# Forming du*B of five scan units on GpSimd instead of TensorE, with their decays in PSUM

## What is computed

```python
x = einsum('bld,ed->bel', ctx, in_proj_w)             # 256 channels
u = silu(conv4(x) + conv_b)                           # causal, 4 taps, by channel
dt_low, B, C = split(einsum('bdl,ed->bel', u, x_proj_w), [8, 24])   # 8 + 16 + 16 rows
dt = softplus(dt_low @ dt_proj_w + dt_proj_b);  A = -exp(A_log)
state = state * exp(dt * A) + (dt * u) * B            # 16 states a channel, 256 steps
y = sum_n(state * C) + D * u;  y = y * silu(layernorm(x))
x = x + tanh(g0) * y.T
xq = quant(layernorm(x));  x1, x3 = split(xq @ w13.T)     # 2 x 704
g = relu(x1)**2 * x3;  out = quant(rmsnorm(g) * w) @ w2.T
x = x + tanh(g1) * out
```

## Time and profile before

| | before |
|---|---|
| time, median of 3 runs | 194.64 us (194.52 to 195.98) |
| the profiled execution, its own time | 194.72 us |
| its span | 192.8 us |
| TensorE matmul busy | 165.3 us, 86% |
| ScalarE busy | 146.8 us, 76% |
| VectorE busy | 145.1 us, 75% |
| GpSimd busy | 109.9 us, 57% |
| chain that ended last | TensorE 56%, VectorE 21%, ScalarE 11%, issue 9%, DMA 2% |

### The profile page before, as it was taken

The page is one execution under the profiler, slowest core; times in us unless marked ns, Lnnn a source line. Parts: engine busy times, 40 slices in busy tenths (PEclk is TensorE's granted clock), DMA queues, the critical chain, the costliest instruction groups (busy, mean ns, idle before and its releaser), DMA issues.

```text
span 192.8 us, 3064 instructions
## 1 busy us (share of the span) xinstructions
PE 165.3 (86%) x1010; PEld 128.1 (66%) x1010; DVE 145.1 (75%) x210; ACT 146.8 (76%) x342; POOL 109.9 (57%) x72
## 2 busy tenths in 40 slices
...
GB/s 123 368 39 202 370 336 12 212 335 58 159 6 129 201 87 188 242 256 21 67 309 247 137 7 178 39 114 0 0 2 29 0 3 0 31 0 27 27 57 55
...
## 3 DMA queue, kind: packets, MB, share of 16 engines
...
q10 hardware_dynamic: 288, 0.16, 0.3%
...
## 4 chain that ended last, share of the span: by engine, by line
PE 56%; DVE 21%; ACT 11%; issue 9%; DMA 2%; DVEq 0%; ACTq 0%
PE m_ps L844 18%; PE w_ps L898 11%; PE y_ps L868 10%; DVE hb L697 9%; PE w_ps L912 8%; DVE xc L642 4%; DVE fam L727 3%; ACT dA L509 2%; ACT sz L497 2%; PE w_ps L803 2%; DMA ctxT<-in_ctxT 2%; PE w_ps L825 1%; PE w_ps L905 1%; ACT xq L548 1%; DVE xstat L621 1%
## 5 line engine op out<-in xcount | busy, mean ns | idle before, releaser
L341 POOL TENSOR_TENSOR hb<-hb,cs 128x1024 f32<-128x1024 f32 x31 | 72.6, 2364 | 22.7 <-DVE hb L697 22.3
L697 DVE TENSOR_TENSOR_SCAN hb<-dA,m_ps 128x1024 f32<-128x1024 f32 x32 | 72.1, 2275 | 17.6 <-PE m_ps L844 5.8
L844 PE MATMUL m_ps<-bd,duT 128*128 128x256 f32 (+1 forms) x224 | 62.7, 422 | 9.3 <-issue 9.3
L509 ACT ACTIVATE dA<-dt,nega 128x255 f32<-128x255 f32 (+1 forms) x160 | 58.9, 451 | 5.2 <-DVE hb L697 5.2
L844 PEld LDWEIGHTS m_ps<-bd,duT 128*128 128x128 f32 x224 | 41.5, 195 | 23.1 <-issue 17.6
L868 PE MATMUL y_ps<-identf,hb 128*128 128x128 f32 x256 | 32.8, 278 | 0.0
L898 PE MATMUL w_ps<-wparts,xqT 128*128 128x352 bf16 x192 | 30.8, 313 | 1.4 <-DVE ffn L740 1.4
L868 PEld LDWEIGHTS y_ps<-identf,hb 128*128 128x128 f32 x256 | 29.7, 143 | 2.5 <-issue 1.4
L898 PEld LDWEIGHTS w_ps<-wparts,xqT 128*128 128x128 bf16 x192 | 18.5, 98 | 12.3 <-DVE ffn L740 1.9
L355 POOL TENSOR_TENSOR ffn<-ffn,normw 128x704 f32<-128x704 f32 x7 | 11.8, 1680 | 23.8 <-DVE ffn L740 23.8
L642 DVE SCALAR_TENSOR_TENSOR xc<-w_ps,sm,xc 128x255 f32<-128x255 f32 (+2 forms) x24 | 11.1, 478 | 7.7 <-ACT xc L474 7.1
...
## 6 DMA issues: line engine op xcount, KB each, us to landing
cs<-c_rows SPq DMA_DIRECT2D x16, 512.0 KB, 5.7
bd<-b_diag SPq DMA_DIRECT2D x12, 512.0 KB, 4.8
...
```

What stands on the lines that cost most here:

```text
L341: E.tensor_tensor(h_g, h_g, cs[:, s0:s0 + sn, l0:l0 + ln], ALU.mult).then_inc(hc_end if (b, i, h) == OUT_END else hc_ok[h], 1)
L509: last = act_fn(dA_g[:, s, 1:ln], dt[:, b, h, l0 + 1:l0 + ln], ACT.Exp, scale=nega[:, h, s0 + s:s0 + s + 1])
L697: V.tensor_tensor_scan(hb[:, k % 3, h], dA[:, k % 2, h].rearrange("p n l -> p (n l)"), m_ps[:, h], 0.0, ALU.mult, ALU.add).then_inc(scan_o ...
L844: last = T.matmul(m_q[:, :, c * P - l0:(c + 1) * P - l0], duT[:, p, c, h * P:(h + 1) * P], bd[:, (s0 + sn // 2 * q) // GN, c, n0:n0 + sn / ...
```

## The change

Five units, 1.3, 2.2, 2.3, 3.1 and 3.3, are made otherwise ("spread" units; `DIAG` says how many groups of four states of a batch keep their diagonals). For them `bget` reads rows of B, repeated on all partitions, from a new DRAM tensor that a new step `rput` writes; a new step `mul0`/`mul1` on GpSimd multiplies them with du into dA (SBUF), `decay` writes its exponentials into m_ps (PSUM), and the scan takes its two operands from the exchanged places. There is no `mix` for them. `bput` writes fewer elements. The first-column zeros are also written in every spread unit and in a unit whose buffer a spread one had two units before.

The orders of all engines are new. What else they hold: the six slices of weight parts are made earlier (most before the first `out`), and their loads stand at the head of SP's queue; `bd/0.1` and `xmr` stand before the first scan; `z` follows one table load; the first table load stands before the first `tap`; `warm` has six steps (8 + 10 transposes before `inproj/0.0`, 8 before `xdbl/0.0`, 8 + 8 before `duT/0.0`, 8 before `inproj/2.0`); the table set named for softplus is another. The number of bf16 parts of the weights stays three.

```diff
-WARM = (10, 8, 8, 8)
+WARM = (10, 8, 8, 8, 8, 8)
 NWP = 6
 WCOL = (0, 704, 1408, 2112, 2816, 3584, 4352)
 CROW, BROW = 32, 64
 LOWC = BROW + NS
-TABLES = ("silu_and_others", "softplus_and_others", "natural_log_exp_and_others", "silu_and_others",
-          "softplus_and_others", "natural_log_exp_and_others")
+TABLES = ("silu_and_others", "softplus", "natural_log_exp_and_others", "silu_and_others",
+          "softplus", "natural_log_exp_and_others")
...
+DIAG = (4, 3, 2, 2)
+
+
+def spread_unit(k):
+
+
+    b, i = divmod(k, NG)
+    s0, sn = group(b, i)[2:]
+    return b >= 0 and s0 // GN >= DIAG[b]
+
+
+def rows_put(b):
+
+
+    return sum(DIAG[c] < NG for c in range(b % 2, b + 1, 2))
+
+
+def mixed(k):
+
+
+    return sum(not spread_unit(j) for j in range(k + 1))
+
+
 PLAN = {
     "pe": """
+        warm/0.1 warm/0.0 inproj/0.0 inproj/0.1 inproj/1.0 warm/0.2 xdbl/0.0 bT/0.0 dtproj/0.0 dtproj/0.1 warm/0.3
+        warm/0.4 duT/0.0 duT/0.1 bT/0.1 xdbl/1.0 mix0/0.0 mix1/0.0 warm/0.5 inproj/2.0 skip/0.0 mix1/0.1 mix0/0.1
+        mix1/0.2 inproj/3.0 mix0/0.2 sum0/0.0 mix1/0.3 sum1/0.0 sum0/0.1 mix0/0.3 xdbl/2.0 dtproj/1.0 xdbl/3.0
...
     "act": """
+        tab/0.0 tap/0.0 tap/0.1 tap/1.0 w_hi/0.0 u/0.0 w_hi/0.1 u/0.1 w_mid/0.0 u/1.0 w_mid/0.1 tab/0.1 soft/0.0
+        soft/0.1 w_hi/0.2 tab/0.2 nega/0.0 duT/0.0 w_mid/0.2 decay0/0.0 w_hi/0.3 xrs/0.0 duT/0.1 decay1/0.0 w_hi/0.4
+        w_mid/0.3 decay1/0.1 w_hi/0.5 tap/2.0 decay0/0.1 w_mid/0.4 decay1/0.2 decay1/0.3 decay0/0.2 tap/3.0 decay0/0.3
+        tab/0.3 z/0.0 z/1.0 u/2.0 gates/0.0 z/2.0 w_mid/0.5 z/3.0 u/3.0 tab/0.4 soft/1.0 soft/2.0 soft/3.0 tab/0.5
+        duT/1.0 szT/0.0 decay0/1.0 decay1/1.0 decay1/1.1 decay0/1.1 decay0/1.2 edge/3.0 szT/1.0 xn/0.0 rs1/0.0
...
     "dve": """
+        conv/0.0 conv/0.1 conv/1.0 lowc/0.0 bd/0.0 du/0.0 du/0.1 xstat/0.0 bd/0.1 lowc/1.0 xmr/0.0 scan1/0.0 scan0/0.0
+        scan1/0.1 scan0/0.1 scan1/0.2 conv/2.0 scan0/0.2 conv/3.0 lowc/2.0 lowc/3.0 scan0/0.3 scan1/0.3 scan0/1.0
+        scan1/1.0 scan0/1.1 yz/0.0 x1/0.0 scan1/1.1 scan0/1.2 scan1/1.2 scan0/1.3 scan1/1.3 fam/0.0 scan1/2.0
+        scan0/2.0 scan1/2.1 scan0/2.1 yz/1.0 x1/1.0 gate/0.0 scan1/2.2 scan0/2.2 gate/0.1 gate/0.2 fam/1.0 gate/0.3
...
     "pool": """
+        w_res/0.0 w_res/0.1 diag/0.0 w_lo/0.0 w_res/0.2 w_lo/0.1 w_lo/0.2 w_res/0.3 w_res/0.4 w_lo/0.3 w_res/0.5
+        out0/0.0 out1/0.0 out0/0.1 w_lo/0.4 out1/0.1 out1/0.2 out0/0.2 w_lo/0.5 du/1.0 du/2.0 out0/0.3 out1/0.3
+        out0/1.0 out1/1.0 out0/1.1 mul0/1.3 mul1/1.3 out1/1.1 out1/1.2 out0/1.2 du/3.0 out0/1.3 out1/1.3 out1/2.0
+        mul1/2.2 mul1/2.3 mul0/2.2 mul0/2.3 out0/2.0 gated/0.0 out0/2.1 out0/2.2 gated/0.1 out1/2.1 out1/2.2 out0/2.3
+        out1/2.3 mul0/3.1 out1/3.0 out0/3.0 gated/1.0 mul1/3.1 out0/3.1 gated/1.1 out1/3.1 mul1/3.3 out1/3.2 mul0/3.3
+        gated/2.0 out0/3.2 gated/2.1 out0/3.3 gated/3.0
     "sp": """
+        l_ctx/0.0 l_w/0.0 l_w/0.1 l_x/0.0 l_w/0.2 cput/0.0 cget/0.0 cget/0.1 dzero/0.0 rput/1.0 cget/0.2 cget/0.3
+        cput/1.0 bput/1.0 cget/1.0 cget/1.1 bget/1.0 cget/1.2 l_nw/0.0 bget/1.1 rput/2.0 cput/2.0 bget/1.2 cget/1.3
+        bget/1.3 cget/2.0 bput/2.0 bget/2.0 bget/2.1 cget/2.1 rput/3.0 bput/3.0 bget/2.2 bget/2.3 bget/3.0 bget/3.1
...
+        def await_m(eng, k, h):
+
+
+            if spread_unit(k):
+                eng.wait_ge(mul_ok[h], k + 1 - mixed(k))
+            else:
+                eng.wait_ge(m_full[h], mixed(k))
+
+        def products_of(b, k, h):
+
+            return states(dA[:, k % 2, h].rearrange("p n l -> p (n l)"), b, k % NG)
+
+        def in_psum(b, k, h):
+
+            return states(m_ps[:, h], b, k % NG)
 
...
+            elif name in ("mul0", "mul1"):
+                k, h = b * NG + i, int(name[-1])
+                l0, ln, s0, sn = group(b, i)
+                for g in c_groups(b, i):
+                    eng.wait_ge(b_got[g], 16 * b)
+                eng.wait_ge(du_ok, b + HALVES)
+                eng.wait_ge(scan_ok[h], k - 1)
+                rows = bd[:, s0 // GN:(s0 + sn) // GN].rearrange("p g c n m -> p (g c n m)").rearrange("p (n l) -> p n l", l=L)
+                E.tensor_tensor(products_of(b, k, h), rows[:, :, l0:l0 + ln],
+                                du[:, p, h, l0:l0 + ln].unsqueeze(1).broadcast_to([P, sn, ln]),
+                                ALU.mult).then_inc(mul_ok[h], 1)
...
-                        for g in range(NG):
+                        for g in range(DIAG[b - 1]):
                             sp.wait_ge(b_got[g], 16 * (b - 1))
                     with nc.allow_non_contiguous_dma("one element of the diagonal per token and state"):
                         for c in range(HALVES):
-                            sp.dma_start(d_diag[:, c, :], low[BROW:BROW + NS, p, c * P:(c + 1) * P]).then_inc(b_put, 16)
+                            sn = GN * DIAG[b]
+                            sp.dma_start(d_diag[0:sn, c, :], low[BROW:BROW + sn, p, c * P:(c + 1) * P]).then_inc(b_put, 16)
+                elif name == "rput":
+                    sp.wait_ge(free["dve"], emptied("xdbl", b, 0))
+                    sp.dma_start(r_dram[b], low[BROW:BROW + NS, p, :]).then_inc(r_put[p], 16)
+                elif name == "bget" and i >= DIAG[b]:
+                    sp.wait_ge(r_put[p], 16 * rows_put(b))
+                    for h in range(HALVES):
+                        await_m(sp, NG * (b - 1) + i, h)
+                    sp.dma_start(bd[:, i].rearrange("p c n m -> p (c n m)").rearrange("p (n l) -> p n l", l=L),
+                                 r_dram[b, GN * i:GN * (i + 1), :].unsqueeze(0).broadcast_to([P, GN, L])
+                                 ).then_inc(b_got[i], 16)
                 elif name == "bget":
                     sp.wait_ge(b_put, 16 * HALVES * b)
                     for h in range(HALVES):
-                        sp.wait_ge(m_full[h], NG * (b - 1) + i + 1)
+                        await_m(sp, NG * (b - 1) + i, h)
                     sp.dma_start(bd[:, i], d_rows[:, :, GN * i:GN * (i + 1), :]).then_inc(b_got[i], 16)
...
+                    spread_k = spread_unit(k)
                     if k >= 2:
-                        act.wait_ge(scan_ok[h], k - 1)
+                        act.wait_ge(scan_ok[h], k if spread_k else k - 1)
                     l0, ln, s0, sn = group(b, i)
-                    dA_g = states(dA[:, k % 2, h].rearrange("p n l -> p (n l)"), b, i)
-                    if b == BATCH - 1 and i < 2:
+                    dA_g = in_psum(b, k, h) if spread_k else products_of(b, k, h)
+
+                    if spread_k or spread_unit(k - 2) or (b == BATCH - 1 and i < 2):
                         act_fn(dA_g[:, :, 0], identf[:, 0:sn], ACT.Copy, scale=0.0).then_inc(cut_ok, 1)
...
-                        first_col = states(m_ps[:, h], b, i)[:, :, 0]
+                        first_col = (products_of if spread_unit(k) else in_psum)(b, k, h)[:, :, 0]
                         dve.wait_ge(carry_ok[h], i - 1)
                         link(V.tensor_tensor(first_col, first_col, carry[:, h, s0:s0 + sn], ALU.add))
-                    V.tensor_tensor_scan(hb[:, k % 3, h], dA[:, k % 2, h].rearrange("p n l -> p (n l)"),
-                                         m_ps[:, h], 0.0, ALU.mult, ALU.add).then_inc(scan_ok[h], 1)
+                    sbuf = dA[:, k % 2, h].rearrange("p n l -> p (n l)")
+                    decays, inputs = (m_ps[:, h], sbuf) if spread_unit(k) else (sbuf, m_ps[:, h])
+                    V.tensor_tensor_scan(hb[:, k % 3, h], decays, inputs, 0.0, ALU.mult, ALU.add).then_inc(scan_ok[h], 1)
```

More of the change, by code:

```diff
@@ L94 @@
+        xqT/3.1 quant2/3.0 relu/3.2 relu/3.3 iqT/3.0 square/3.1 rs2/3.1 quant2/3.1 iqT/3.1
     """,
     "dve": """
-        conv/0.0 conv/0.1 conv/1.0 lowc/0.0 bd/0.0 du/0.0 du/0.1 xstat/0.0 lowc/1.0 scan1/0.0 scan0/0.0 bd/0.1
-        scan1/0.1 scan0/0.1 conv/2.0 scan0/0.2 scan1/0.2 xmr/0.0 conv/3.0 scan1/0.3 lowc/2.0 lowc/3.0 scan0/0.3
-        scan0/1.0 scan1/1.0 scan0/1.1 yz/0.0 x1/0.0 scan1/1.1 scan0/1.2 scan1/1.2 fam/0.0 scan0/1.3 scan1/1.3
-        scan0/2.0 scan1/2.0 scan0/2.1 scan1/2.1 scan0/2.2 gate/0.0 yz/1.0 x1/1.0 scan1/2.2 gate/0.1 gate/0.2 fam/1.0
@@ new lines @@
+        scan0/2.3 absmax/0.0 absmax/0.1 scan1/2.3 gate/1.0 gate/1.1 scan0/3.0 scale2/0.0 scan1/3.0 gate/1.2 gate/1.3
+        outscale/0.0 yz/2.0 x1/2.0 scan0/3.1 absmax/1.0 fam/2.0 scan1/3.1 scan0/3.2 final/0.0 scan1/3.2 absmax/1.1
+        yz/3.0 final/0.1 x1/3.0 scale2/1.0 gate/2.0 fam/3.0 gate/2.1 scan1/3.3 gate/2.2 gate/2.3 outscale/1.0
+        scan0/3.3 final/1.0 absmax/2.0 absmax/2.1 scale2/2.0 out1/3.3 gate/3.0 gate/3.1 yz/3.1 x1/3.1 outscale/2.0
+        fam/3.1 final/1.1 absmax/3.0 scale2/3.0 final/2.0 outscale/3.0 gate/3.2 gate/3.3 gated/3.1 absmax/3.1
@@ L106 @@
+        scale2/3.1 outscale/3.1 final/2.1 final/3.0 final/3.1
     """,
     "pool": """
[L108 to L111 removed]
```

74 lines of the change are left out of this document (29 added, 45 removed).

## The result

The kernel after takes 186.87 us (median of 4 runs, 185.95 to 188.96), the one before 194.94 beside it: a ratio of 0.956, with a 95% interval of 0.950 to 0.962. Timed once more with the experiments it took 188.09, ratio 0.965 (0.959 to 0.971). The forecast was 184.2 with a range of 178 to 194. In what follows a median counts all runs of a kernel, while a ratio leaves out the executions in the chip's slower state and one each of outscale_gpsimd and before_xmr that took 847 and 928 us, and where too few are left there is no ratio.

The account below looks back on a forecast made before the run. TensorE was taken to bound the second half, VectorE's scans the first. From a span of 192.8, start -2.5, middle -5.0 and tail -3.0 gave 182.3, plus 1.9 around the span: 184.2 us, range 178 to 194.

Parts of the forecast that it names:

- TensorE relieved: Behind the first scan of batch 1, ten mixes fewer take 17.3 us off TensorE; its busy time falls from 116.3 to 99.
- mul at 2.36 us: Ten new GpSimd products at 2.36 us each, 23.6 in all, bounds 1.2 and 4.7 each; GpSimd's middle goes to 90.0.
- The rival in which GpSimd becomes the bound: GpSimd's ten mul make it slower than before; break-even at 3.5 us each. Slower, mostly this rival: 0.08.
- Decays into PSUM: ScalarE's exponentials written to PSUM cost the same as to SBUF, bounds 0.1 us an instruction either way, 5.6 us in all.
- The decays in line: A spread unit's decay waits for the scan before it and can't run ahead: 1 us in all, bounds 0 and 4.
- The start, -2.5: Up to the first scan of batch 1, which comes at 60.8 and not 63.3: -2.5 us, bounds +2 and -7.
- The `xmr` chain: In the start: small VectorE instructions with port waits, taken at 4.4 us, moved ahead of the first scan.
- The middle, -5.0: From 63.3 to 168.2 us: -8 TensorE waits, +3.5 port, +1 decays, -1.5 other waits; -5.0, bounds +3 and -10.
- the port: Small VectorE instructions with two SBUF inputs wait for GpSimd's product under way: 3.5 us more, bounds 0 and 10.
- the prediction's signs of being wrong: mul over 3.5 us, first scan of batch 1 behind 63, or VectorE's middle idle time merely released by ScalarE or GpSimd.
- The second rival: Work moves but not the end: start even, port loses 8 to 10 us, tail gives 2; near 192.7, chance 0.12.
- The tail, -3.0: Behind the last product with C: 5.5 us less TensorE work, the last batch's own sequence stays; -3.0, bounds 0 and -5.

Follow-up runs that it names:

- outscale_gpsimd: The kernel after with the outscale chain of batches 0 and 1 done by GpSimd, not VectorE: 182.0 us, ratio 0.929 to the kernel before.
- before_xmr: The kernel before with bd/0.1 and xmr ahead of the first scan, xrs behind duT/0.1, orders otherwise kept: 194.0 us, ratio 0.992.
- before_tables: The kernel before with the other softplus table set and the first table load ahead of the first tap: 195.1 us, ratio 0.994.
- all_diag: The kernel after with the spread units undone (all mixes on TensorE, no mul or rput), all else kept: 191.8 us, ratio 0.981 to the kernel before.
- spread_only: The kernel before with the five spread units put into its own orders, tables and ten warm transposes: 230.9 us, no ratio.

## Why the prediction was right, step by step

The time was in the range, 2.7 us from the forecast, and the direction and its reason (TensorE relieved, paid on other engines) held. But two of its three terms were mis-sized by more than that (by 4.5 and 8.2 us, in opposite directions) and cancelled; that the sum came so near is luck.

- **TensorE relieved:** right. 64 mix records fewer, and none of VectorE's waits left on it. Its busy time behind the first scan of batch 1 was put at 99 us and is 106.1, since other work now stands behind that scan too.
- **mul at 2.36 us:** right, 2.360. GpSimd's middle was put at 90.0 us and is 88.9. The rival in which GpSimd becomes the bound needed 3.5 us a piece, and falls.
- **Decays into PSUM:** four exponentials of 128x255 take 1.65 us as before. As the Trainium skill, page "ScalarE: Activation LUTs", section "Step-by-step: what each stage is for", has it, the single instruction is shorter into PSUM (457 against 499 ns), but the next one starts no earlier, so the term is nil, as taken. The decays in line (1 us taken) can't be told apart: `L577` waited 9.7 us in the middle for scans (four times), and VectorE 0.3 us for a decay.
- **The start, -2.5:** it was -7.0, the edge of its bounds. Two numbers in it failed. The `xmr` chain was carried over with its 4.4 us, though 2.3 of those were waits behind GpSimd that the new place does not have. The slow rate of the first projections was carried over too, though behind the transposes they ran at the later rate (eight records in 1.89 us), so the first dt came 0.8 us earlier and not 1 later. So the first scan came at 26.0 and not 30.0, and the taps for batch 3 were through at 38.1 and not 43. From there to the first scan of batch 1 it took 18.2 us, where 17.8 were added up, so ScalarE's sequence was right. Of the table loads, charged at 1.28 us each, before_tables shows 1.3 us in all.
- **The middle, -5.0:** it was +3.2. The failed step is the port: "I take 3.5 us more (about two waits), bounds 0 and 10". VectorE's small instructions took 15.1 us more. With that in the place of 3.5 the sum gives +6.6, so not all of it reached the end. The mechanism was named, with the chain of `outscale` in it, but the size came from counting occasions and not links. In the middle of the kernel before four instructions waited over 1 us; in the kernel after twelve do (three fam, three finv, two gt, four links of one outscale chain), at 1.8 us each, beside a GpSimd that is busy for 82% of the middle. It was also laid to GpSimd's larger share, while all_diag shows 8.8 of the 15.1 us without one `mul`, by the new orders alone: what counts is which step meets a product. None of the prediction's signs of being wrong would have caught it: VectorE's idle time of 16.9 us did not change its releaser but fell to 4.7 and became busy time. The second rival, with 8 to 10 us at the port, was nearer here than the forecast, and was wrong on the start and the tail instead.
- **The tail, -3.0:** it was -4.0, and all of it is order: every kernel with the new orders has 20.6 or 20.7, with or without spread units. The 5.5 us of TensorE work that the prediction took out of it (5.4 by the stretches) it charged nowhere, though they now stand in the middle.
- **Additive thinking:** the sum treated the orders and the spread units as separate gains. all_diag and spread_only show that neither carries over: the orders, tables and `warm` alone give 1.9% (1.0 to 2.7), the spread units alone in the old orders cost 17%.
